# Moving the output projection and the feed-forward part of a transformer layer one sequence later in the pipeline

## The reference

```python
qkv = x @ qkv_w + qkv_b                        # 16 heads of 16
local = _local_attention(heads(q), heads(k), heads(v))     # window of 128 keys, softmax
pooled = x.reshape(B, nlat, chunk, D).mean(axis=2)         # 64 latent tokens
remote = softmax(mask(rq @ rk.T)) @ rv @ rout_w + rout_b
gate = sigmoid(local @ gl_w + remote_h @ gr_w)
mixed = gate * local + (1.0 - gate) * remote_h
x = _layernorm(x + mixed @ out_w + out_b)
x_norm = x / (rms(x) + 1e-8)
h = gelu(x_norm @ ternary(w_up).T)             # width 1024, erf form
x = _layernorm(x + (h / (rms(h) + 1e-8)) @ ternary(w_down).T)
```

## Time and profile before

| | |
|---|---|
| median of 3 runs | 1309.5 us (1309.12 to 1319.59) |
| profiled execution, its own time | 1306.51 us |
| its span, first to last instruction | 1304.8 us |
| granted TensorE clock, mean of the span | 0.922 |
| PE busy | 1071.0 us (82%) |
| DVE busy | 963.8 us (74%) |
| POOL busy | 686.1 us (53%) |
| ACT busy | 666.2 us (51%) |

### The profile page before, as it was taken

The page is one execution under the profiler, slowest core; times in us unless marked ns, Lnnn a source line. Parts: engine busy times, 40 slices in busy tenths (PEclk is TensorE's granted clock), DMA queues, the critical chain, the costliest instruction groups (busy, mean ns, idle before and its releaser), DMA issues.

```text
span 1304.8 us, 37906 instructions
## 1 busy us (share of the span) xinstructions
PE 1071.0 (82%) x15776; PEld 685.5 (53%) x15776; DVE 963.8 (74%) x2048; ACT 666.2 (51%) x1026; POOL 686.1 (53%) x870
## 2 busy tenths in 40 slices
PE   2566889798988989897998989899888989795855
PEld 1344555464655556464655556465555646464533
DVE  5856768778787887878787877878787887866445
ACT  1213555564646556464646556364655556462624
POOL 6542637373654736364554637265473737364553
PEclk9778989899998999899999989899998989997887
DMA  5845180735537181644628082543719173541000
GB/s 153 139 79 110 43 139 30 125 64 91 92 75 123 37 134 48 115 82 76 107 66 132 30 136 54 106 76 76 122 44 137 46 120 69 98 68 35 2 18 17
DMA packets 57019, 108.08 MB, mean 83 GB/s; under 512 B 14192, under 2 KB 40944, under 8 KB 53744
## 3 DMA queue, kind: packets, MB, share of 16 engines
q1 hardware_dynamic: 56848, 105.66, 44.1%
HBM read 71.55 MB, written 34.08 MB: 81 GB/s over the span
## 4 chain that ended last, share of the span: by engine, by line
PE 52%; DVE 28%; ACT 9%; issue 4%; POOL 4%; SPq 1%; DMA 1%; DVEq 0%; POOLq 0%; ACTq 0%
PE work L1477 9%; PE oacc L1405 7%; PE oacc L1424 6%; PE work L1230 5%; PE work L1348 5%; PE scores L1385 3%; DVE x L1058 3%; PE work L1415 3%; ACT Pt L760 3%; DVE x L1066 3%; DVE nmax L1000 2%; PE scores L1230 2%; DVE ytok L1134 2%; DVE Pt L966 2%; DVE lat_st L963 2%
## 5 line engine op out<-in xcount | busy, mean ns | idle before, releaser
L760 ACT ACTIVATE Pt<-scores 128x1024 f32<-128x1024 f32 (+1 forms) x256 | 228.3, 914 | 115.4 <-PE oacc L1405 83.2
L626 POOL TENSOR_TENSOR h_lo<-hbuf,h_hi 128x512 f16<-128x512 f32 x128 | 148.3, 1159 | 249.6 <-DVE h_hi L1114 249.6
L1000 DVE TENSOR_REDUCE nmax<-work 128x3 f32<-128x480 f32 x352 | 216.5, 636 | 27.8 <-PE work L1353 23.9
L598 POOL TENSOR_SCALAR_AFFINE_SELECT Pt<-Pt 128x512 f32<-128x512 f32 x256 | 163.2, 638 | 109.6 <-ACT Pt L760 108.1
L1477 PE MATMUL work<-xnT,wup_t 128*128 128x512 f16 x512 | 156.6, 444 | 32.5 <-DVE xnT L1102 32.1
L1348 PE MATMUL work<-Ks,Qs 98*32 98x160 bf16 x4096 | 141.5, 237 | 33.0 <-DVE nmax L1000 28.7
L1405 PE MATMUL oacc<-Pt,Vp 128*32 128x256 f32 (+1 forms) x2048 | 149.6, 359 | 3.5 <-POOL Pt L602 3.0
L1255 PE MATMUL scores<-xT,wqk 128*128 128x512 f32 x256 | 116.5, 609 | 19.3 <-ACT xT L695 19.3
L1385 PE MATMUL scores<-Qs,Ks 100*32 100x160 bf16 (+4 forms) x4096 | 113.7, 228 | 13.5 <-ACT Pt L760 10.1
L602 POOL TENSOR_SCALAR_AFFINE_SELECT Pt<-Pt 128x512 f32<-128x512 f32 x192 | 122.0, 635 | 0.0
L1424 PE MATMUL oacc<-wdn_t,h_hi 128*128 128x256 f16 x512 | 120.2, 276 | 0.2
(11 more groups left out here) (169 smaller groups left out, 2088.8 us busy)
## 6 DMA issues: line engine op xcount, KB each, us to landing
parts_scratch<-parts SPq DMA_DIRECT2D x96, 256.0 KB, 6.8
Qs<-parts_scratch SPq DMA_DIRECT2D x96, 256.0 KB, 9.2
Ks<-parts_scratch SPq DMA_DIRECT2D x96, 256.0 KB, 8.9
xtok<-L_attn_x SPq DMA_DIRECT2D x16, 512.0 KB, 13.7
xres<-L_attn_x SPq DMA_DIRECT2D x16, 512.0 KB, 14.8
y<-ytok SPq DMA_DIRECT2D x16, 512.0 KB, 3.2
Qs<-L_ffn_w_up SPq DMA_DIRECT2D x1, 1024.0 KB, 5.6
Qs<-L_ffn_w_down SPq DMA_DIRECT2D x1, 1024.0 KB, 7.6
```

The costliest lines, as they stand in the source:

```text
L598: ins = pool.affine_select(out=pt[:, :, 0:P], in_=pt[:, :, 0:P], compare_op=ALU.is_gt, fill=0.0, base=0, pattern=[[0, 4], [1, P]], channel ...
L626: pool.tensor_tensor(h_lo[:, t % NR, :], hbuf[:, t % 2, :], h_hi[:, t % NR, :], ALU.subtract).then_inc(h_lo_ready, 1)
L760: nc.scalar.activation(Pt[:, u % NPT, :, 0:w], scores[:, slot, :, :].rearrange("p k (h q) -> p (k h) q", h=2)[:, :, 0:w], ACT.Exp, scale=S ...
L1000: nc.vector.tensor_reduce(nmax[:, :, :].rearrange("p b h -> p (b h)")[:, first:first + n], work[:, slot, 0:n * BAND].rearrange("p (h c) -> ...
```

## The change

Body s now finishes sequence f = s-1 instead of s, and there is one more body (17). The output projection and the first norm of f (MIX_T, OUT, STATS, NORM, NORM_X, XN_T, XN_HI, XN_LOW) move into the first half, between the attention steps of s, by the table EARLY. The eight UP steps and END of f stay in the second half; only the gate of s itself stays there too, as steps "G". The steps of a projection's three-way split that come after the first get their own entries "R" in the table. The exponential of the gate and those of the latent scores stand ahead of the first Gelu on ACT (SCALAR_HALF moves UP and UP+1 behind LAT_SCORES+1 on ACT alone).

Work also changes engine: ACT makes h_hi with a second Gelu from PSUM instead of DVE's cast; ACT copies the transposed xn to SBUF (xnF), casts from there (XN_HI), and POOL makes the low part that DVE made; POOL adds the two parts of `mixed`, and makes lat_bd. The second norm's statistics come as one piece at the end of the second half ("L", `last_stats`) instead of a piece per step. ytok has two buffers, mixed its own.

```diff
+MIX_T, OUT, STATS, NORM, NORM_X, XN_T, XN_HI, XN_LOW = 0, 2, 4, 5, 6, 7, 9, 11
+EARLY = {1: [MIX_T], 2: [MIX_T + 1], 4: [OUT], 5: [OUT + 1], 6: [STATS], 8: [NORM], 9: [NORM_X],
+         12: [XN_T], 13: [XN_T + 1], 14: [XN_HI], 15: [XN_HI + 1, XN_LOW], 16: [XN_LOW + 1]}
 SECOND_HALF = (
-    ("P", X_T), ("F", GATE), ("P", QK), ("F", MIX), ("P", QK + 1), ("P", QK + 2), ("P", QK + 3),
...
+    ("G", GATE_MIX), ("F", UP + 2), ("R", 3), ("P", VALUES), ("F", UP + 3), ("P", LAT_NORM),
...
+SCALAR_HALF = tuple(x for x in SECOND_HALF if x not in (("F", UP), ("F", UP + 1)))
+SCALAR_AT = SCALAR_HALF.index(("P", LAT_SCORES + 1)) + 1
+SCALAR_HALF = SCALAR_HALF[:SCALAR_AT] + (("F", UP), ("F", UP + 1)) + SCALAR_HALF[SCALAR_AT:]
...
+def attention_step(u):
+    order = [("S", u + 1)] if u + 1 < NU else []
+    order += [("A", v) for v in A_OF[u][:1]]
+    order += [("E", k) for k in EARLY.get(u, [])]
+    order += [("V", u - 2)] if u >= 2 else []
+    order += [("A", v) for v in A_OF[u][1:]]
...
 def over_sequences(body):
-    for i in range(B):
-        body(Seq(i, i % 2, i // 2))
+    for i in range(B + 1):
+        body(Seq(i))
```

On POOL, the gate:

```diff
-                if k == GATE:
+                if k == GATE_MIX:
                     pool.wait_ge(gate_g, count(s, 1, 0))
                     for b in range(NB):
                         rv = rem[:, s.par, b, 0:D].rearrange("p (h d) -> p h d", h=H)
                         pool.tensor_tensor(rv, rv, gate[:, 2, b, :].unsqueeze(2).to_broadcast([P, H, HD]),
                                            ALU.mult).then_inc(rem_part, 1)
+                        pool.wait_ge(rem_part, count(s, NB, b))
+                        pool.wait_ge(mixed_part, count(s, NB, b))
+                        pool.tensor_tensor(mixed[:, b, :], mixed[:, b, :], rem[:, s.par, b, 0:D], ALU.add
+                                           ).then_inc(mixed_ready, 1)
```

On ACT, a step UP+t:

```diff
-                    gelu = nc.scalar.activation(hbuf[:, t % 2, :], work[:, slot, :], ACT.Gelu)
+                    nc.scalar.activation(hbuf[:, t % 2, :], work[:, slot, :], ACT.Gelu).then_inc(h_act, 1)
+                    if t >= NR:
+                        act.wait_ge(down_done, count(s, FT, t - NR))
+                    nc.scalar.activation(h_hi[:, t % NR, :], work[:, slot, :], ACT.Gelu).then_inc(h_hi_ready, 1)
```

On DVE, a step UP+t:

```diff
-                    nc.vector.tensor_copy(h_hi[:, t % NR, :], hbuf[:, t % 2, :]).then_inc(h_hi_ready, 1)
```

On DVE, where the projection's pooled sums are made, and the walk through the second half:

```diff
-                if k == QK:
+                if k == (QK if s.i < 2 else QK + 1):
...
                 for phase, k in SECOND_HALF:
-                    if phase == "F":
-                        f_step(s, k)
-                    elif later.exists:
+                    if phase == "F" and f.exists:
+                        f_step(f, k)
+                    if phase == "G" and s.exists:
+                        gate_step(s, k)
+                    if phase == "P" and later.exists:
                         p_step(later, k)
+                    if phase == "L" and f.exists:
+                        last_stats(f)
```

More of the change, by code:

```diff
@@ L488, in body @@
                     load_x(later)
[L489 to L492 removed]
+                if s.i >= 2:
+                    store(Seq(s.i - 2))
+                if s.exists:
+                    load_xres(s)
+                if s.next().exists:
                     move_max(s.next())
@@ L755, in weights @@
                     act.wait_ge(pv_done, count(s, NU, u - NPT))
-                if u == 1 and not s.last:
+                if u == 1 and s.next().exists:
                     act.wait_ge(part2, count(s.next(), 4, 3))
@@ L811, in body @@
                         copy_o(s, (u - 6) // NB)
-                    if not s.last:
+                    if s.next().exists:
                         for t in range(2):
@@ L1372, in scores_T @@
                 slot, k = score_use(s, u)
-                if u < 2 and not s.last:
+                if u < 2 and s.next().exists:
                     for bank in (2 * slot, 2 * slot + 1):
```

580 lines of the change are left out of this document (304 added, 276 removed).

## The result

| | before | after |
|---|---|---|
| median of 4 runs each, same chip | 1309.3 us (1305.8 to 1319.6) | 1496.1 us (1491.1 to 1500.4) |
| ratio, 95% interval | | 1.143 [1.135, 1.150] |
| profiled execution, own time | 1306.5 us | 1492.0 us |
| granted TensorE clock | 0.922 | 0.879 |

The kernel is 14% slower. I had forecast slower, 1416 us, with a range up to 1465: the direction is right, the size is 80 us short and outside the range.

The account below looks back on a forecast made before the run. No engine is full, so the order of waits decides. Halves of 33.3 and 47.4 us make 80.7 a body, thirteen 1049.1; with first and last bodies 1396.9, plus 18 for the clock: span 1415, time 1416 us, range 1340 to 1465.

Parts of the forecast that it names:

- UP+2: Second half: PE waits 3.05 us for UP's bank, which table load, two Gelus and a Square must free.
- h_sum 2: Second half: h_sum of UP+2 stands behind the gate's products on DVE; PE waits 2.6 us for UP+4's bank.
- h_lo 2: Second half: third h_lo stands behind POOL's eight gate operations, down of block 2 behind it; PE waits 3.1 us.
- rem at the seam: End of second half: next body's first scores need rem's banks; PE has nothing from 44.4 to 47.4.
- step 10 and 11: First half: PE waits 2.7 us for max_low's bank, then exponential 10, which follows norm and xn copies.
- The clock: Lower clock in PE's dense stretch of the second half: half of 2.7 us, 1.35 a body, 18 over 13.
- PE's own work: PE's work by pitches, start to start: 19.4 us in a first half, 39.3 in a second, 58.7 a body.
- Transfers: K stack's reads end 45 us after X_T, next body needs them at 48: hidden, by 3 us only.
- The two rules of the Trainium skill: Counter-arguments: table-load drain of 1380 ns, 18 us more; DVE and POOL excluding each other, 1.7 us more a body.
- A: Rival, faster: POOL's and ACT's blocks find cover, PE bounds a body at 66 us; some 1190 us; chance 0.16.
- B: Rival, no change: half of the new waits hide, 74 us a body, 1300 to 1325 us; chance 0.12.
- D: Rival: the order on ACT doesn't keep the tables apart; two loads a body seen, so given nothing.

Follow-up runs that it names:

- e17: Changed kernel with half of the K stack's reads left out from the third sequence on, other rows keeping old values; 1491.0 us, ratio 1.145 to before.
- e3: Changed kernel with the latent output and both remote steps ahead of the last feed-forward step; 1491.2 us, ratio 1.145 to before.
- e4: Changed kernel with TensorE doing the product UP+4 and the scores of step 10 twice; 1496.2 us, ratio 1.149 to before.
- e6: Changed kernel with both halves of the maxima ahead of the norm in step 9, and ACT's xn copies in two pairs; 1481.7 us, ratio 1.132 to before.
- e2: Changed kernel with POOL's eight gate operations spread, two behind each of four lower parts of h; 1472.1 us, ratio 1.130 to before.
- e5: e2 with DVE's gate values and products moved to right behind the latent scores; 1440.4 us, ratio 1.100 to before.
- e14: Changed kernel with e3, e5, e6, query/key chunk 3 ahead of the Gelus, all values ahead of UP+2, xn copies in steps 10 to 13; 1414.9 us, ratio 1.085.
- e16: e14 with half of the K stack's reads left out from the third sequence on, other rows keeping old values; 1380.1 us, ratio 1.061 to before.
- e1: Changed kernel with the norm of x1 at step 10 instead of 9; 1485.1 us, ratio 1.141 to before.

## Why the prediction was wrong in size and right in direction

The span is 1490.0, the working gave 1396.9 without the clock. The 93 between them, by the X_T starts shown above (forecast 143.9, 215.2, 1183.6):

- **Body 0 starts at 120.0 as before: wrong, 6.4 us.** It starts at 126.41, and its X_T is 7.1 late. The change also moves the making of lat_bd to POOL in the prologue, where it stands behind a reduction over all partitions (at 47.08): PE waits 12.92 us for it at 55.85. The prologue was not walked.
- **The bridge to body 1's X_T: 79.7 us instead of 71.3, 8.4 us.** PE waits 11.99 there for the K stack and loses 5.8 to the clock. With half of the stack's reads left out (e17) the bridge takes 74.4.
- **Twelve bodies at 85.64 instead of 80.7: 59.3 us.** The main part, below.
- **From body 13's X_T to the end: 231.7 instead of 213.3, 18.4 us.** The same blocks as in a body; PE loses 25 us to the clock there. Not taken apart further.

Against these 93 stood 18 for the clock: 75 us short.

**The waits: the right ones, and 5 us too many.** Forecast 22.0 a body (80.7 - 58.7), measured 16.6 in body 6 and 17.0 on average over twelve ((1027.66 - 823.40) / 12). In the second half: pooled 1.5 (1.45), UP+2 3.05 (2.90), h_sum 2 2.6 (0.99 in this body, 2.4 in e3's), h_lo 2 3.1 (2.81), last h_sum 0.3 (0.24), rem at the seam 3.0 (2.94). The times were worked out from durations in the trace of before alone. In the first half: step 10 and 11 2.7 (3.15, all of it for the maxima at step 10; the exponential of step 11 is in time), step 8 1.35 (0.97), 0.9 for MIX_T and OUT (0.6). The 1.3 at the start for the second norm's statistics is missing; PE does its first score and maxima groups at half clock there, which may cover it. Of the 1.55 in smaller ones 0.5 was found. So the sum of the first half's waits, 7.8, should have been 5.3.

**The clock: the term that was mis-sized.** The prediction put 1.35 us a body ("half of 2.7"), for one stretch behind UP's wait, as before. There are four in body 6, and PE loses 7.6 us in that body, 7.5 on average over the twelve (3.7 before): 6.15 more than forecast, 12 x 6.15 = 74 us. I had counted one wait ahead of one dense stretch, where the walk itself gave four waits of about 3 us, each with dense work behind it. In this body each of them is followed by half clock; those of 1.5 us and less are not. That a stretch goes when its wait goes is not shown one by one: in e3 a wait of the same length took the place of the one removed, and e4 filled too little. That the clock's share counts for the time is shown by three pairs where it fell while the idle time stood still: from the changed kernel to e6, from e2 to e5 and from e14 to e16. These figures say where PE's time went; they are not what a higher clock would give back. The first half was taken at 25.5 us of work; without its 5.3 of waits it took 31.6.

**PE's own work: 58.7 was too low.** 85.34 - 16.6 - 7.6 leaves 61.1, which is also the average of the twelve. The same arithmetic for the body of before gives 73.87 of the earlier trace rows less 9.36 of idle time (23.41 - 21.32 and 50.46 - 43.19) and 2.8 of clock: 61.7. So all of the 2.4 by which 58.7 falls short was there before, and my sum of pitches left it out: what it called 15.6 of waits and clock was 12.2.

Together, on average: -5.0 for the waits, +7.5 for the clock of which the sum had none, +2.4 for the work, which is the 4.9 between 80.7 and 85.64. Of the 11.4 us by which the average body grew (85.64 from 74.22), 8.3 are PE's waits (17.0 from 8.7) and 3.8 the clock (7.5 from 3.7), less 0.6 of the rest. So most of the slowdown is waiting, as forecast; what the forecast missed of it is the clock.

**Transfers: hidden, as forecast, and by less.** The K stack was put at 45 us behind X_T. In e3, where nothing else holds the seam, the maxima start when it lands, at 711.70, 49.4 behind X_T at 662.35; the rem wait covers it in the changed kernel. e17 shows that it costs nothing there, e3 that it costs 3.1 as soon as rem does not.

**The two rules of the Trainium skill.** The drain of 1380 ns that the Trainium skill ("ScalarE: Activation LUTs", section "What ACT_TABLE_LOAD costs") adds to a table load is not in this trace, which now shows a Gelu ready to go:

```profile
675.26 1.28 ACT L859 ACT_TABLE_LOAD   x1
676.56 0.60 ACT L859 ACTIVATE hbuf<-work 128x512 f32<-128x512 f32 x1
```

The Gelu starts 0.02 us behind the load, so nothing of the 18 us that the rule would have added is seen. The rule of the Trainium skill on DVE and POOL ("SBUF — State Buffer", section "Who interferes with whom") would have made POOL's eight operations 7.8 us, by my estimate; with DVE's products (2.81 us) beside the first of them they took 6.0, near the 6.1 that the rows gave.

**Rivals.** A (PE bound, 1190) would need the blocks to find cover; taking them away one after the other gave 1415 at best, because the K stack and then DVE's maxima stand behind them (e16). B and D did not come. No version here beats the kernel before: e14 is at 1.085, and e16, which leaves data out, at 1.061. Against before, e14 has 77 us more of idle time and 32 more lost to the clock. What of the old order the deeper pipeline lacks, so that the old one stays ahead of e14, was not settled by a run.

## What to carry to other kernels

Walk the in-order queues of all engines with the durations of the trace: it gave five of the six waits of the second half within 0.3 us. Then look behind each wait of about 3 us for dense TensorE work and put in the clock for every such pair, not once a body, and walk the prologue with the same diff. Keep three sums apart in every run (idle, lost to the clock, the rest): e6 against the changed kernel, e5 against e2 and e16 against e14 won their time in the second while the first stood still; e3 against the changed kernel lost 20 us less in the second and was no faster. When experiments take a wait away and the time stays, look for the same block under its next name before giving up the theory: e1, e2 and e3 gained 16 us at most, e5 with two blocks gone 55.
